# Routing of a post-norm MoE layer on one core: fewer VectorE steps per tile, six count products on TensorE, one subtraction moved to GpSimd

## The reference, cut to what matters

```python
x = layernorm(x + attention(x))                     # 2048 tokens x 512, 16 heads
logits = x @ gate_w.T                               # 64 experts
scores = softmax(logits)
gate_vals, idx = top_k(scores, 6)
onehot = fe[:, None] == arange(E)[None, :]          # fe: the chosen experts, token by token
pos = take_along_axis(cumsum(onehot) - 1, fe)       # the place of a choice in its expert
keep = pos < 128                                    # capacity
buf[fe, pos] = ft                                   # rows of x gathered for each expert
h = silu(xe @ w1.T) * (xe @ w3.T);  ye = h @ w2.T   # per expert, 352 wide
routed = sum over k of ye[fe, pos] * gate_vals
z = shared expert on every token (704 wide)
out = layernorm(x + routed + z)
```

## Time and profile before

| | us |
|---|---|
| median of 3 runs | 2611.55 (2609.22 to 2616.04) |
| the profiled execution | 2612.08 |
| its span | 2610.3 |
| routing stage in it | about 1664 to 1952 |
| busy over the span: PE, DVE, ACT, POOL | 2474.8, 1762.7, 1454.5, 268.6 |

### The profile page before, as it was taken

The page is one execution under the profiler, slowest core; times in us unless marked ns, Lnnn a source line. Parts: engine busy times, 40 slices in busy tenths (PEclk is TensorE's granted clock), DMA queues, the critical chain, the costliest instruction groups (busy, mean ns, idle before and its releaser), DMA issues. The chain is left out here.

```text
span 2610.3 us, 40937 instructions
## 1 busy us (share of the span) xinstructions
PE 2474.8 (95%) x14304; PEld 2141.0 (82%) x14304; DVE 1762.7 (68%) x3802; ACT 1454.5 (56%) x3247; POOL 268.6 (10%) x221
## 2 busy tenths in 40 slices
PE   6999999999999999999999999798899999999992
PEld 5888888888888888888888888576688889898992
DVE  4666566566566557557567566588867888888884
ACT  3555555455456456456456455444436777777771
POOL 0000000000000000000000000045551112122121
PEclk9999999999999999999999999899999999999996
DMA  6311311310320320311311220367749999999995
GB/s 250 124 49 47 120 49 47 123 51 15 118 88 15 108 86 27 108 54 55 108 58 55 82 66 18 144 219 269 248 134 278 308 295 317 305 299 318 303 310 154
DMA packets 176892, 380.09 MB, mean 146 GB/s; under 512 B 19561, under 2 KB 52457, under 8 KB 166448
## 3 DMA queue, kind: packets, MB, share of 16 engines
q1 hardware_dynamic: 154096, 330.69, 37.4%
q0 software_dynamic: 20288, 42.59, 7.1%
q10 hardware_dynamic: 2304, 4.20, 0.4%
HBM read 279.67 MB, written 106.35 MB: 148 GB/s over the span
## 5 line engine op out<-in xcount | busy, mean ns | idle before, releaser
L402 ACT ACTIVATE pT_hi<-turned 128x512 fp32r<-128x512 f32 (+3 forms) x640 | 330.4, 537 | 292.1 <-PE turned L623 291.1
L495 DVE TENSOR_TENSOR pT_lo<-turned,pT_hi 128x512 fp32r<-128x512 f32 (+3 forms) x640 | 375.5, 604 | 104.9 <-ACT pT_hi L402 102.9
L391 ACT ACTIVATE probs<-bank,neg_max 128x512 f32<-128x512 f32 (+3 forms) x640 | 395.9, 626 | 80.2 <-DVE neg_max L489 76.1
L481 DVE TENSOR_REDUCE max_part<-bank 128x1 f32<-128x512 f32 (+2 forms) x576 | 344.8, 621 | 114.5 <-PE bank L606 103.7
L593 PE MATMUL bank<-x_sb,w_hi 128*128 128x512 f32 x1024 | 323.4, 397 | 20.1 <-ACT ident_bf L366 13.6
L623 PE MATMUL turned<-ident,probs 128*128 128x128 f32 x2176 | 320.5, 273 | 0.3 <-PEq L682 0.3
L623 PEld LDWEIGHTS turned<-ident,probs 128*128 128x128 f32 x2176 | 263.1, 141 | 44.9 <-issue 0.7
L638 PE MATMUL z_ps<-pT_hi,v_hi 128*128 128x512 f32 (+3 forms) x640 | 255.6, 399 | 14.9 <-DVE pT_lo L495 12.4
L606 PE MATMUL bank<-k_lo,q_hi 128*128 128x512 f32 (+2 forms) x640 | 254.2, 397 | 0.0
L606 PE MATMUL bank<-k_hi,q_hi 128*128 128x512 f32 (+2 forms) x640 | 250.3, 391 | 0.0
L1736 DVE TENSOR_TENSOR up_lo<-w_raw,up_hi 128x704 fp32r<-128x704 f32 x256 | 217.3, 887 | 34.3 <-ACT up_hi L1243 33.3
(11 more groups left out here) (211 smaller groups left out, 5259.4 us busy)
## 6 DMA issues: line engine op xcount, KB each, us to landing
w_raw<-in_w SPq DMA_DIRECT2D x256, 352.0 KB, 5.6
x_sb<-x_parts SPq DMA_DIRECT2D x62, 1024.0 KB, 6.0
w_raw<-in_w SPq DMA_DIRECT2D x128, 256.0 KB, 5.7
gathered_x<-empty_row SPq DMA_DIRECT2D x64, 263.5 KB, 9.3
rows_in<-gathered_x SPq DMA_DIRECT2D x64, 263.5 KB, 5.4
z_dram<-z_sb SPq DMA_DIRECT2D x64, 256.0 KB, 2.3
z_raw<-z_dram SPq DMA_DIRECT2D x16, 1024.0 KB, 5.8
w_raw<-in_w_qkv SPq DMA_DIRECT2D x32, 384.0 KB, 10.5
```

The costliest lines, as they stand in the source:

```text
L391: nc.scalar.activation(probs[:, u % 2, r, kc * CHUNK:kc * CHUNK + used], bank[:, job_at["s", h, c, r, kc] % BANKS, 0:used], ACT.Exp, bias= ...
L402: nc.scalar.activation(pT_sb[0][:, n % TURNS, lo_col:], turned[:, n % TURNS, lo_col:], ACT.Copy).then_inc(turn_hi, 1)
L481: nc.vector.reduce_max(max_part[:, row % ROWS, kc:kc + 1], bank[:, job % BANKS, 0:used], axis=AX_X).then_inc(part_done, 1)
L495: nc.vector.tensor_tensor(pT_sb[1][:, n % TURNS, lo_col:], turned[:, n % TURNS, lo_col:], pT_sb[0][:, n % TURNS, lo_col:].bitcast(F32), AL ...
```

## The change

- `choose` no longer sums the 64-wide one-hot rows of the six choices and casts the sum; the one-hot `pick` is written as bf16 (double-buffered), and TensorE multiplies each of the six slices. The counts stay in PSUM over all tiles: for tile k, six products of `rest_bf` (ones on and below the diagonal) complete the counts of tile k-1, and six of `before_bf` add those of tile k.
- Gates: ScalarE takes the exponentials of the six sorted values (`top_e`) instead of VectorE's product and sum over 6 x 64.
- The low part of the turned x1 is made on GpSimd from the copy in SBUF, behind the `moved` wait of the scatter two tiles earlier; each scatter begins with an iota that writes the token numbers.
- `normalise` is split: `measure` (sum, variance), then `choose` of the tile before, then the inverse root, which has two steps less.
- On TensorE the counts stand after head 9 and not 14; on ScalarE the shared piece is split ahead of `turned_x1`.

```diff
-    LATE = (12, 14)
+    COUNTED, TURNED = 9, 12
...
+            def split_x1T(k):
+                pool.wait_ge(t_hi, done(0, k))
+                pool.wait_ge(t_read, done(0, k))
+                if k >= 2:
+                    pool.wait_ge(t_stored[k % 2], 32 * (k // 2))
+                nc.gpsimd.tensor_tensor(xT_part[1][:, k % 2], x1T[:, k % 2], xT_part[0][:, k % 2].bitcast(F32),
+                                        ALU.subtract).then_inc(t_split, 1)
+
             def scatter(k):
+                if k >= NB:
+                    pool.wait_ge(x1_stored[k % NB], 16 * (k // NB))
                 wait_apart(pool, waited, placed, done(0, k))
+                nc.gpsimd.iota(x1[:, k % NB, TOKEN:TOKEN + 1].bitcast(I32), pattern=[[0, 1]], base=k * P,
+                               channel_multiplier=1).then_inc(token_made, 1)
+                pool.wait_ge(token_made, k + 1)
                 for n in range(TOPK):
                     nc.gpsimd.indirect_dma_start(
...
             for k in range(AHEAD):
                 split_shared(k)
                 load_shared(k + 1)
+                if k:
+                    split_x1T(k - 1)
             for k in range(TILES):
                 scatter(k)
+                if k + 2 < TILES:
+                    split_x1T(k + 2)
                 if k + AHEAD < SHARED_PARTS * NP:
                     split_shared(k + AHEAD)
...
             def exponentials(i, k):
-                act.wait_ge(l_read, done(i, k))
-                nc.scalar.activation(ex[:], lg_c[:], ACT.Exp, accum_out=small[:, 4:5]).then_inc(exp_ready, 1)
+                act.wait_ge(topped, done(i, k))
+                nc.scalar.activation(ex[:], lg_c[:], ACT.Exp, accum_out=small[:, 4:5])
+                nc.scalar.activation(top_e[:], top[:, 0:TOPK], ACT.Exp).then_inc(exp_ready, 1)
...
                     split_z(i, k + 1)
+                if k < SHARED_PARTS * NP:
+                    split_shared(k)
                 if exists(i, k - 1):
                     turned_x1(i, k - 1)
-                if k < SHARED_PARTS * NP:
-                    split_shared(k)
...
             def counts(i, k):
-                pe.wait_ge(chosen_ready, done(i, k))
                 if exists(i, k - 1):
                     pe.wait_ge(c_read, done(i, k - 1))
-                nc.tensor.matmul(c_ps[:, 0], before_bf[:], chosen_bf[:], start=True, stop=True)
-                nc.tensor.matmul(c_ps[:, 1], ones_bf[:], chosen_bf[:], start=True, stop=True).then_inc(c_ready, 1)
+                    for n in range(TOPK):
+                        nc.tensor.matmul(c_ps[:], rest_bf[:], pick[:, (k - 1) % 2, n], start=False, stop=False,
+                                         skip_group_check=True)
+                pe.wait_ge(chosen_ready, done(i, k))
+                for n in range(TOPK):
+                    mark = nc.tensor.matmul(c_ps[:], before_bf[:], pick[:, k % 2, n], start=not exists(i, k - 1) and n == 0,
+                                            stop=n == TOPK - 1, skip_group_check=True)
+                mark.then_inc(c_ready, 1)
...
             def step(i, k):
+                if exists(i, k - 1):
+                    measure(i, k - 1)
+                if exists(i, k - 2):
+                    choose(i, k - 2)
                 if exists(i, k - 1):
                     normalise(i, k - 1)
-                if exists(i, k - 2):
-                    choose(i, k - 2)
                 if exists(i, k + 1):
                     split_z(i, k + 1)
                 if exists(i, k - 2):
                     route_gates(i, k - 2)
-                if exists(i, k - 1):
-                    split_x1T(i, k - 1)
-                if exists(i, k - 2):
                     places(i, k - 2)
```

More of the change, by code:

```diff
@@ L811, in route_and_experts @@
             top = sb("top", [P, 8], stack=first)
-            top_e = sb("top_e", [P, 8], stack=first)
+            top_e = sb("top_e", [P, TOPK], stack=first)
             idx = sb("idx", [P, 8], U32, first)
-            pick = sb("pick", [P, TOPK, EXPERTS], stack=first)
+            pick = sb("pick", [P, 2, TOPK, EXPERTS], BF16, first)
             pick_pos = sb("pick_pos", [P, TOPK, EXPERTS], stack=first)
[L816 to L819, removed]
             slot = sb("slot", [P, 2, TOPK], U32, first)
@@ L826, in route_and_experts @@
             before_bf = sb("before_bf", [P, P], BF16, first)
-            ones_bf = sb("ones_bf", [P, P], BF16, first)
+            rest_bf = sb("rest_bf", [P, P], BF16, first)
         s_up.append([sb(f"s_up_{n}1", [P, DT, 2 * INTER], F32R) for n in ("hi", "lo")])
@@ L857, in route_and_experts @@
             l_ps = ps("l_ps", [P, EXPERTS], stack=first)
-            c_ps = ps("c_ps", [P, 2, EXPERTS], stack=first)
+            c_ps = ps("c_ps", [P, EXPERTS], stack=first)
         h_even = ps("h_even", [P, 2, CHUNK])
@@ L901, in route_and_experts @@
         l_read = sem("l_read")
+        topped = sem("topped")
         exp_ready = sem("exp_ready")
@@ L986, in _ @@
                                     base=0, pattern=[[1, P]], channel_multiplier=-1).then_inc(pool_const, 1)
+            nc.gpsimd.affine_select(out=rest_bf[:], in_=rest_bf[:], compare_op=ALU.is_ge, fill=0.0,
+                                    base=0, pattern=[[-1, P]], channel_multiplier=1).then_inc(pool_const, 1)
             nc.gpsimd.iota(mine_i[:], pattern=[[1, NE]], base=0, channel_multiplier=0).then_inc(pool_const, 1)
@@ L1402, in step @@
                 if exists(i, k):
-                    project(i, k, range(0, LATE[0]))
+                    project(i, k, range(0, COUNTED))
+                if exists(i, k - 2):
+                    counts(i, k - 2)
+                if exists(i, k):
+                    project(i, k, range(COUNTED, TURNED))
                 if exists(i, k - 1):
@@ L1406, in step @@
                 if exists(i, k):
-                    project(i, k, range(LATE[0], LATE[1]))
-                if exists(i, k - 2):
-                    counts(i, k - 2)
-                if exists(i, k):
-                    project(i, k, range(LATE[1], HEADS))
+                    project(i, k, range(TURNED, HEADS))
                 if exists(i, k - 1):
@@ L1635, in choose @@
                 wait_apart(dve, waited, l_read, done(i, k))
[L1636 to L1637 removed]
+                nc.vector.max(top[:], lg_c[:]).then_inc(topped, 1)
+                wait_apart(dve, waited, topped, done(i, k))
+                link(nc.vector.max_index(idx[:], top[:], lg_c[:]), apart=True)
                 idx_f = x1[:, k % NB, CHOICES:CHOICES + 8]
                 link(nc.vector.tensor_copy(idx_f, idx[:]))
[L1640 to L1641 removed]
+                if exists(i, k - 1):
+                    dve.wait_ge(c_ready, done(i, k - 1))
+                nc.vector.tensor_tensor(
+                    pick[:, k % 2], iota_f[:].rearrange("p (k e) -> p k e", k=1).to_broadcast([P, TOPK, EXPERTS]),
                     idx_f[:, 0:TOPK].rearrange("p (k e) -> p k e", e=1).to_broadcast([P, TOPK, EXPERTS]),
[L1643 to L1645 removed]
+                    ALU.is_equal).then_inc(chosen_ready, 1)
+                dve.wait_ge(chosen_ready, done(i, k))
+                dve.sem_inc(route_chain, 1)
+                made[route_chain] += 1
                 assert made[route_chain] == CHOOSE_STEPS, made[route_chain]
@@ L1803, in _ @@
             nc.vector.memset(eps[:], EPS).then_inc(dve_const, 1)
-            nc.vector.memset(ones_bf[:], 1.0).then_inc(dve_const, 1)
-            nc.vector.memset(count[:], 0.0).then_inc(dve_const, 1)
-            dve.wait_ge(dve_const, 3)
+            dve.wait_ge(dve_const, 1)
             split_z(0, 0)
```

70 lines of the change are left out of this document (28 added, 42 removed).

## The result

The changed kernel takes 2626.78 us (median of 7 runs, 2624.44 to 2632.45), the kernel before beside it 2609.22 (7 runs): the ratio is 1.0063, with a 95% interval of 1.0049 to 1.0076, some 16 us slower. The forecast was 2624. The profiled execution took 2624.44 with a span of 2622.7.

What follows compares the result with a forecast made beforehand. GpSimd's queue was taken to bound the routing stage; 21.8 + 5.6 - 2.7 - 10.2 - 3 = +11.5 us on the profiled 2612.08 gave 2623.6, said as 2624 us, range 2603 to 2643.

Steps and rivals of the forecast that it cites:

- The bound: Routing stage: GpSimd's queue, a chain of 232.5 us from first scatter to first addition, trails and sets the stage's end.
- the 2.6 us: Stage end: TensorE's stand of 2.61 us for VectorE's reading, held by GpSimd, taken as the time TensorE had to spare.
- rival D: More than the sum: port meetings, or ScalarE's split waiting for its load ahead of the turned x1; 2646 us, chance 0.13.
- The subtractions: Fourteen new subtractions on GpSimd behind the waits for landing, 1.56 us each, add 21.8 us.
- The iota: An iota at the start of each scatter on GpSimd, with its wait, 0.35 us for each of 16, adds 5.6 us.
- The start: First slots ready about 3 us sooner, with a subtraction ahead of GpSimd's first scatter: 2.7 us saved.
- The waits of the first eleven tiles: GpSimd's waits for rows to land, 3.8 us each, fall from 52.0 to 41.8 us, minus 10.2.
- The two kinds: Landing waits average 2.75 us with z's load issued before the scatter, 6.2 with it issued inside.
- The last five waits: GpSimd's landing waits of the last five tiles: the sum of 17.7 us left unchanged.
- The issues: GpSimd's scatter issues: 3 of the 13 us by which they were longer come off.
- The sum: Routing stage: 21.8 + 5.6 - 2.7 - 10.2 - 3 = +11.5 us, and the bodies start that much later.
- What was to be worth nothing: About 4.0 us a step off VectorE: worth nothing at the stage's end; some 24 us were GpSimd not there.

Runs made afterwards that it cites:

- x1t_twice: The changed kernel with each subtraction for the low part of x1 made twice on GpSimd: 2643.69 us, ratio 1.0128 to the kernel before.
- x1t_before_landing: The changed kernel with GpSimd's subtraction placed between a tile's last scatter issue and the wait for its rows: 2603.60 us, ratio 0.9971 to the kernel before.
- vector_act_back: The changed kernel with x1's low part back on VectorE and ScalarE turning x1 ahead of the shared split, as before: 2599.70 us, ratio 0.9954.
- x1t_alone: The kernel before with only the subtraction for x1's low part moved to GpSimd: 2629.45 us, ratio 1.0071 to the kernel before.
- act_order_back: The changed kernel with ScalarE turning x1 ahead of the split of a shared piece, as before: 2627.13 us, ratio 1.0057 to the kernel before.
- the late wait: GpSimd waits for a tile's rows only just ahead of the next tile's scatter: 2614.68 us on the kernel before, 2588.85 on the changed kernel.
- x1t_on_vector: The changed kernel with x1's low part back on VectorE, ScalarE's new order kept: 2615.77 us, ratio 1.0023 to the kernel before.
- before_land_late: The kernel before with GpSimd waiting for a tile's rows only just ahead of the next tile's scatter: 2614.68 us, ratio 1.0013.

## Why the prediction was right

- **The bound.** That time in GpSimd's queue is time of the stage is shown by x1t_twice and x1t_before_landing. The reason given for the end isn't right: the 2.6 us were to show that nothing but GpSimd is late there, but 1.98 of them are the ordinary turn from product to reading to product and stay without GpSimd. TensorE had 0.6 us to spare and about none after, so by this trace its own lateness, which ScalarE's stands for GpSimd's loads make, counts about as much. The prediction's sum had the queue act through its end; the path by the loads stands only in its rival D.
- **The subtractions** behind the landings: 22.5 us, predicted 21.8.
- **The iota**: 3.2, predicted 5.6. The instruction cost 0.15 us and its wait 0.28, but in ten tiles the gap of 0.30 behind the load went, and only the difference counts there. This term was mis-sized.
- **The start**: 1.5 us earlier against the stage's own start (49.5 us for 51.1), predicted 2.7.
- **The waits of the first eleven tiles**: 45.2 (8.03, 5.16, 5.10, 4.21, 3.15, 5.23, 3.34, 4.01, 2.46, 2.70, 1.81), predicted 41.8. The size was near, the picture was not. z's load was to be issued ahead of every scatter; it was in four tiles (waits 2.5 to 5.1, mean 3.5) and inside the scatter in six (1.8 to 5.2, mean 3.9). The two kinds no longer differ by a factor of two, and why they don't stays open. Nor does the reason hold that the new subtraction, by delaying SyncE's store, shortens these waits: in vector_act_back, without it in the queue, the same eleven sum to 45.4.
- **The last five waits**: 12.8, predicted unchanged at 17.7. This step failed; what shortened them no run isolates, and in every other run they sum to 14.4 or less.
- **The issues**: 1.6 less, predicted 3. The eleven pieces, for which nothing was set, took 1.4 more.
- **The sum**: +12.1 on the stage in the profiled executions, predicted +11.5; by medians of seven runs +17.6, by the ratio 16. The two profiled executions lay on different sides of their medians (2.9 over before, 2.3 under after), and the forecast was set on one of them. That the stage came within 1 us is in part luck: what was set too low (the first eleven waits by 3.4, the issues by 1.4, the pieces by 1.4, the start by 1.2, the subtractions by 0.7) cancels against what was set too high (the last waits by 4.9, the iota by 2.4).
- **What was to be worth nothing** on VectorE was worth next to nothing here: 2 us from x1t_alone to act_order_back. That the relief would pay 24 us were GpSimd not there came near to what the late wait shows (26), though from a kernel that the late wait itself had made no faster.
- **Rival D**'s ScalarE half was present, as 20.9 us of waiting for the turned x1. The new order itself cost nothing that act_order_back could return; what ScalarE's stands for the loads cost no run isolates. Its condition (the front behind GpSimd's scatters) came true in x1t_on_vector. As to meetings, two of the fourteen subtractions (3.34 and 3.41 us) stood behind a `z_lo`, and two `z_lo` (3.34 and 3.20) behind a subtraction. Here the trace agrees with what the Trainium skill (SBUF — State Buffer, "Who interferes with whom") states of the pair; how often they meet only the run tells.

## What to carry to other kernels

A queue that waits for its own transfers has free time only ahead of the wait: the same subtractions cost 23 us more behind it than in front of it. A queue that lags can hold the others at a place far from its end, here by the loads that it issues. Before an engine is relieved, find the one that trails; relief of any other shows up as idle time there, and is paid out only when the trailing one is shortened. And an experiment that says "this doesn't matter" holds for the bound of that kernel: ScalarE's order was worth nothing and 16 us in two kernels that differ in one subtraction's place.

## What the runs showed of the hardware

Two kinds of meeting were larger than expected. An indirect DMA's issue on GpSimd, 0.98 us alone, took 2.34 us at 1805.91 and at 1841.33 in the changed kernel, each begun 0.8 us into a `z_lo` of 2.28 us, and 2.97 beside VectorE's `z_lo` in before_land_late. And a VectorE subtraction of 6 elements took 2.40 us for 0.17, begun 0.63 us before GpSimd's of 1.73: it ended with it, though the trace has it begin first. Such a meeting can repeat from tile to tile once two queues run in step: the `slot` rows of 1791.10, 1807.32, 1823.77 and 1840.31 took 2.38 to 2.40 us each.

Of TensorE's clock: in the changed kernel TensorE stood 8.27 us for a turned x1, and the eight products behind took 1.97 us for 1.00 elsewhere. The granted clock over just these products is 0.50 (third number from the end), which is 1.2 GHz and not 2.4.

```profile
1762.19 1.97 PE L1428 MATMUL l_ps<-gw,x1T 128*128 128x64 f32 x8 [8.27 <-ACT x1T L1227]
...
1762.19:1764.16 1.97, 1.97 (x9) 1.97 (x10) 0.00 (x0) 1.94 (x3) 0.00 (x0) 0.50 1.02 399
```

The window around it has a mean granted clock of 0.72, the next one 1.00. In the kernel before, which had no such long stands, it was 0.96 over the 130 us shown above, for 0.91 here. The slower products come on top of each long wait. From GpSimd's first instruction of the stage to its own first unit of the shared expert TensorE took 13.7 us more than before (254.6 for 240.9), of which 7.3 are idle time; how the rest divides between the lower clock and the added count products, and whether the clock moved the end, no run shows.

```profile
1760.00:1775.00 15.00, 12.81 (x59) 10.59 (x60) 9.18 (x20) 7.34 (x11) 8.41 (x9) 0.72 0.71 241
1775.00:1790.00 15.00, 15.00 (x85) 12.40 (x84) 10.49 (x22) 6.20 (x9) 9.29 (x9) 1.00 0.69 245
```
